# Three products of key halves, a partly on-chip tail and a reordered transition in a cross-attention and stream-mixing kernel

## Chip, cores and metric

The kernel runs on one core of a Trainium2 chip. The metric is the device time of one execution in microseconds (us). Its engines are PE (TensorE, matrix products, with its weight loads listed apart as PEld), DVE (VectorE), ACT (ScalarE), POOL (GpSimd) and SP (SyncE, which here issues every DMA).

## What is computed

For 16 batches of x and ctx, each 256 rows (channels) by 2048 columns, all in float32:

```
x = x + xattn(layernorm(x), ctx)      # layernorm over the 2048 columns
  qh = Wq x ; kh = Wk ctx ; vh = Wv ctx            # 512 = 8 heads of 64
  qh = softmax over the 64 of a head ; kh = softmax over the 2048 columns
  out = Wo (heads' context^T qh) + bo ; x += out / norm(out) * g * 16
x = x + ffn(layernorm(x))             # every row is 4 streams of 512
  24 logits a row (W_res, W_pre, W_post), 50 Sinkhorn rounds on the 4x4 part
  y = (sum of streams * pre) @ W_branch
  out = H_res mixed streams + post * y
```

## The kernel before

The batches are done one behind the other (`for b in range(NB)`), and each batch has a written-out order of **places** that all five engine programs walk through. A batch has 32 key places, `("A", b, r, i)` and `("B", b, r, i)` for r = 0..3 (a block of 128 of the 512 key channels) and i = 0..3 (a quarter of 512 columns), and then 27 query places `("Q", b, i)`.

In the A places `key_logits` (line 546) makes the logits of one quarter, two float32 matmuls of 128x128 by 128x512 into the bank `big[i]`. DVE takes the maxima (`key_max`, line 773, and `key_max_all`, line 780), ACT exponentiates in the B places (`key_exp`, line 1129). PE turns the exponentials round (`key_transpose`, line 557), ACT copies them out (`turn`, line 1138), PE multiplies them by the transposed context (`key_context`, line 571). In the query places follow query logits (line 603), their softmax on DVE, ACT and POOL (lines 857 to 879, 1143, 1346, 1354), transposes (613), the attention product (628), the norm (1154, 887, 1364, 897), the sum with x on POOL (1371) and its return to rows (647, 650, 1161). The key logits of the first block (r = 0) of the next batch are made already in query places 16, 17, 21 and 23; their common maximum is taken behind the last query place and their exponentials in the next batch's B places.

Other work is hung on places by the table `tasks` (`put(place, ...)`): statistics of x (`stat`, line 800; `mean`), the centring of x by ACT (`center`, line 1167) with the scaled weights `wqs` by POOL (line 1330), the small `norm`, `logits` and `pre` steps of the batch before, its branch product y (`y`, lines 1174, 1049, 662, 670), the Sinkhorn steps (`sink`, five groups of 4, 4, 4, 2 and 2 batches), and the `mix`: 24 rows of four streams and y are loaded from DRAM with their coefficients, multiplied by a 121x96 matrix on PE (line 681), copied by ACT (line 1195) and stored. Behind the last batch (place TAIL) come its norm, logits, pre and y, then the Sinkhorn steps of the last group (2 batches, 512 rows) with the mixes still open between them, and then the 22 mixes of this group. Every engine works its program in order, so a wait holds back all that stands behind it on that engine.

## Time and profile before

| | |
|---|---|
| median of 3 runs | 2906.38 us (2905.24 to 2907.76) |
| the profiled execution's own time | 2906.39 us |
| its span, first to last instruction | 2904.7 us |
| mean granted TensorE clock | 0.967 |
| busy: PE / PEld / DVE / ACT / POOL | 2626.9 / 1735.8 / 1663.3 / 1033.0 / 804.3 us |

"L546" is line 546 of the kernel. A row of a group of instructions gives the engine, the operation, the tiles it writes and reads with their shapes, the count, the busy time in us and the mean length of one in ns, and the idle time of the engine ahead of them with what ended it. A row of the timeline gives start and length in us. The names `big`, `tb`, `kc_bank` and `misc` are PSUM banks.

### The profile page before, as it was taken

The numbers are of one execution on the slowest core, as the hardware profiler recorded it, in microseconds if no ns is written. First come the engines' busy times: TensorE is split into PE (matmuls) and PEld (weight loads), VectorE is DVE, ScalarE is ACT, GpSimd is POOL, SyncE is SP. The second block draws the span as 40 slices with busy tenths as digits, with TensorE's granted clock in tenths as the row PEclk, the third lists the DMA queues.
The fourth block names the chain that finished last, engine by engine and source line by source line (L and its number), as shares of the span: only waits on it lengthen the run. The fifth ranks groups of instructions, "written<-read, shape, count | busy, mean of one in ns | idle before, by whom it ended". The sixth has DMA issues, their size and how long they took to land.

```text
span 2904.7 us, 32933 instructions
## 1 busy us (share of the span) xinstructions
PE 2626.9 (90%) x11002; PEld 1735.8 (60%) x11002; DVE 1663.3 (57%) x4194; ACT 1033.0 (36%) x2312; POOL 804.3 (28%) x785
## 2 busy tenths in 40 slices
PE   7989898999989898999989999898998999999765
PEld 4766666666656566565666656566665566656411
DVE  2444434345766757355664766534587685867482
ACT  2333333334332333434333343333434333343222
POOL 1322314050422304142231513214051141512311
PEclk9999999999999999999999999999999999999878
DMA  6112121203112120413324221232413324231166
GB/s 223 37 55 91 58 95 54 92 22 107 39 55 91 59 95 29 140 61 105 120 76 128 70 89 64 82 121 67 137 61 104 122 71 133 69 100 32 52 180 169
DMA packets 203082, 258.22 MB, mean 89 GB/s; under 512 B 45218, under 2 KB 111522, under 8 KB 202914
## 3 DMA queue, kind: packets, MB, share of 16 engines
q1 hardware_dynamic: 202914, 256.12, 28.0%
q8 instruction: 88, 1.44, 0.2%
q14 instruction: 80, 0.66, 0.1%
HBM read 180.17 MB, written 75.89 MB: 88 GB/s over the span
## 4 chain that ended last, share of the span: by engine, by line
PE 77%; DVE 14%; ACT 3%; issue 2%; DMA 1%; POOL 1%; SPq 1%; DVEq 0%; ACTq 0%; POOLq 0%
PE big L628 16%; PE kc_bank L571 15%; PE big L546 13%; PE big L603 13%; PE tb L670 4%; PE tb L613 4%; PE tb L557 4%; PE misc L650 3%; PE tb L681 3%; DVE stats L800 2%; ACT turned L1138 2%; PE kc_bank L647 2%; DVE ska L974 1%; DVE skr L977 1%; DMA out<-mix_out 1%
## 5 line engine op out<-in xcount | busy, mean ns | idle before, releaser
L1138 ACT COPY turned<-tb 128x512 f32<-128x512 f32 x512 | 297.8, 585 | 1021.1 <-PE tb L613 692.7
L546 PE MATMUL big<-ctx_sb,wk 128*128 128x512 f32 x1024 | 515.2, 632 | 50.3 <-ACT k_exp L1129 50.1
L628 PE MATMUL big<-merged,turned 128*128 128x256 f32 x2048 | 492.9, 383 | 61.7 <-ACT turned L1138 61.1
L628 PEld LDWEIGHTS big<-merged,turned 128*128 128x128 f32 x2048 | 380.5, 190 | 206.5 <-issue 123.6
L571 PE MATMUL kc_bank<-ctxt,turned 128*128 128x256 f32 x2048 | 481.8, 379 | 6.8 <-ACT turned L1138 6.8
L603 PE MATMUL big<-wqs,x_sb 128*128 128x512 f32 x1024 | 482.0, 596 | 5.5 <-DVE q_sb L867 4.7
L1346 POOL TENSOR_TENSOR qhalf<-q_sb 128x512 f32<-128x512 f32 x128 | 162.2, 1267 | 922.4 <-ACT q_sb L1143 922.4
L571 PEld LDWEIGHTS kc_bank<-ctxt,turned 128*128 128x128 f32 x2048 | 372.3, 190 | 60.7 <-issue 20.1
L546 PEld LDWEIGHTS big<-ctx_sb,wk 128*128 128x128 f32 x1024 | 195.0, 202 | 246.2 <-issue 173.0
L773 DVE TENSOR_REDUCE kmax<-big 128x1 f32<-128x512 f32 x256 | 173.8, 686 | 286.3 <-PE big L546 285.6
L1354 POOL TENSOR_TENSOR q_sb<-q_sb,qsum 128x1024 f32<-128x1024 f32 x128 | 243.3, 1901 | 332.1 <-DVE qsum L879 332.1
L681 PE MATMUL tb<-mix_ld,mix_w 121*96 121x512 f32 (+2 forms) x346 | 205.7, 690 | 95.9 <-POOL mix_w L1336 66.0
L603 PEld LDWEIGHTS big<-wqs,x_sb 128*128 128x128 f32 x1024 | 180.7, 191 | 155.4 <-issue 145.8
L887 DVE TENSOR_SCALAR nrm<-nrm 128x2 f32<-128x2 f32 x128 | 72.1, 563 | 250.3 <-ACT squares L1154 250.2
L795 DVE TENSOR_SCALAR chain_raw<-kc_bank,ksum 128x256 f32<-128x256 f32 x64 | 31.0, 484 | 314.3 <-PE kc_bank L571 314.0
L857 DVE TENSOR_REDUCE qmax<-big 128x8 f32<-128x512 f32 x256 | 176.3, 689 | 49.1 <-PE big L603 43.4
L867 DVE TENSOR_TENSOR q_sb<-big,qmax 128x512 f32<-128x512 f32 x256 | 169.4, 662 | 52.2 <-PE tb L613 49.7
L1129 ACT ACTIVATE k_exp<-big,kmax 128x512 f32<-128x512 f32 x256 | 175.7, 688 | 53.1 <-DVE kmax L780 53.1
L1371 POOL TENSOR_TENSOR x_tr<-x_tr,on 128x512 f32<-128x512 f32 x128 | 164.7, 1287 | 55.2 <-DVE on L897 55.2
L800 DVE BATCH_NORM_STATS2 stats<-x_sb 128x6 f32<-128x512 f32 x256 | 163.9, 683 | 23.6 <-ACT x_sb L1161 17.0
L1143 ACT ACTIVATE q_sb<-q_sb 128x1024 f32<-128x1024 f32 x128 | 135.4, 1058 | 101.6 <-DVE q_sb L867 101.6
L1195 ACT COPY mix_out<-tb 96x512 f32<-96x512 f32 (+2 forms) x173 | 100.0, 578 | 190.7 <-PE tb L681 140.8
(124 smaller groups left out, 3090.7 us busy)
## 6 DMA issues: line engine op xcount, KB each, us to landing
mix_ld<-streams SPq DMA_DIRECT2D x168, 240.0 KB
ctx_sb<-in_ctx SPq DMA_DIRECT2D x64, 512.0 KB, 9.2
ctxt<-in_ctx_t SPq DMA_DIRECT2D x64, 512.0 KB, 4.6
x_sb<-in_x SPq DMA_DIRECT2D x64, 512.0 KB, 9.0
x_tr<-in_x_t SPq DMA_DIRECT2D x64, 512.0 KB, 6.4
streams<-x_sb SPq DMA_DIRECT2D x64, 512.0 KB, 2.9
out<-mix_out SPq DMA_DIRECT2D x168, 192.0 KB, 2.2
streams<-y_sb SPq DMA_DIRECT2D x32, 256.0 KB, 2.0
```

The lines of the kernel that those rows point to most:

```text
L546: t = nc.tensor.matmul(big[i], wk[:, ct, dt * P:(dt + 1) * P], ctx_sb[b % 2][:, ct, quarter(i)], start=ct == 0, stop=ct == CT - 1)
L571: t = nc.tensor.matmul(kc_bank[:, 0:C], turned[n % 3][:, j * P:(j + 1) * P], ctxt[:, nt, :], start=nt == 0, stop=nt == NT - 1)
L603: t = nc.tensor.matmul(big[i % 2], x_sb[b % 2][:, ct, i * P:(i + 1) * P], wqs[:, ct, :], start=ct == 0, stop=ct == CT - 1)
L628: t = nc.tensor.matmul(big[2 + p % 2][:, half], turned[n % 3][:, dt * P:(dt + 1) * P], merged[:, dt, :], start=dt == 0, stop=dt == DT - 1)
L681: t = nc.tensor.matmul(bank[0:count * STREAMS, :], weights, mix_ld[k][0:ONES + 1, :], start=True, stop=True)
L773: nc.vector.tensor_reduce(kmax[:, 1 + i:2 + i], big[i], AX_X, ALU.max).then_inc(s_kmax, 1)
L800: t = nc.vector.bn_stats(target[:, ct, i, :], x_sb[b % 2][:, ct, quarter(i)])
L857: nc.vector.tensor_reduce(qmax[:, i % 2, :], big[i % 2].rearrange(heads, d=DIM_HEAD), AX_X, ALU.max).then_inc(s_qmax, 1)
L867: nc.vector.tensor_tensor(q_sb[p % QB][:, i % 2, :].rearrange(heads, d=DIM_HEAD), big[i % 2].rearrange(heads, d=DIM_HEAD), qmax[:, i % 2, ...
L1129: nc.scalar.activation(k_exp[:, i * BANK:(i + 1) * BANK], big[i], ACT.Exp, bias=kmax[:, 0:1], accum_out=ksum[:, i:i + 1]).then_inc(s_kexp, 1)
L1138: nc.scalar.copy(turned[k % 3][:], tb[n % 2][:]).then_inc(s_tba, 1)
L1354: nc.gpsimd.tensor_tensor(exps, exps, qsum[:, p % 2, 1, :].unsqueeze(2).broadcast_to([P, 2 * HEADS, DIM_HEAD]), ALU.mult).then_inc(s_qn, 1)
```

## The change

**Key logits.** The weights of the keys and the context are no longer kept in float32: ACT rounds each to a tile of type float32r (`wk_h`, `ctx_h`), POOL subtracts it from the original and keeps the rest, again as float32r (`wk_l`, `ctx_l`). `key_logits` becomes six matmuls: h·h, h·l and l·h for each half of the 256 channels; l·l is left out. The context comes by quarters into two `stage` tiles; loading, rounding and subtracting are tasks of the last key places and of query places 0 to 11.

**Transition.** `key_max_all` of the next batch's first block stands behind its last maximum (query place 24), its first exponential on ACT behind query place 25. The statistics of x move from key places 4 to 7 to 9, 11, 14 and 15, `mean` to 16, `center` to 18 to 27, and `pre` of the batch before to 7, 8 and 9.

**x normalised.** ACT's centring now also multiplies by 1/sigma (`scale=r1`, with `shift1` = -mean/sigma from DVE); POOL's scaling of the query weights (`wqs`) is gone.

**Tail.** The last batch's `pre` and `y` tasks stand between the Sinkhorn steps, one behind every fourth. Of the last group only its first batch goes through the mixes (11 tiles for 22). The last batch is mixed from what is on the chip: ACT makes 8 tiles of 128x512 (`own_first`), DVE adds four terms to each (`own_pair`), SP stores them. `LOADS` goes from 6 to 5.

```diff
-                 for n, size in enumerate(GROUPS)]
-    LOADS, AHEAD = 6, 4
+                 for n, size in enumerate((*GROUPS[:-1], GROUPS[-1] - 1))]
+    LOADS, AHEAD = 5, 4
...
-            put(keys[4 + i], "stat", b, i)
-        put(keys[9], "mean", b)
+            put(keys[(9, 11, 14, 15)[i]], "stat", b, i)
+        put(keys[16], "mean", b)
         for ct in range(CT):
             for i in range(NQ):
-                put(keys[11 + 8 * ct + 2 * i], "center", b, ct, i)
-        put(keys[12], "wq", b)
+                put(keys[(18, 19, 21, 23, 24, 25, 26, 27)[ct * NQ + i]], "center", b, ct, i)
+        put(keys[17], "shift", b)
         if b:
             put(keys[13], "load x_t", b)
         if b + 1 < NB:
             put(keys[25], "load", b + 1)
+
+            for i in range(NQ):
+                put(keys[28 + i] if i < 2 else ("Q", b, 3 * i - 3), "ctx", b + 1, i, -1)
+                for ph in range(1 + CT):
+                    put(("Q", b, 3 * i + ph), "ctx", b + 1, i, ph)
         if b:
-            put(keys[4], "pre", b - 1, 0)
-            put(keys[5], "pre", b - 1, 1)
-            put(keys[6], "pre", b - 1, 2)
+            put(keys[7], "pre", b - 1, 0)
+            put(keys[8], "pre", b - 1, 1)
+            put(keys[9], "pre", b - 1, 2)
             for ct in range(CT):
                 for ph in range(6):
...
+        if n % 4 == 3 and behind_tail:
+            put(TAIL, *behind_tail.pop(0))
...
+                n = b * NQ + i
+                if n >= 2:
+                    w.wait_ge(s_cl, (n - 1) * CT)
+                elif n:
+                    w.wait_ge(s_wkl, 1)
+                nc.sync.dma_start(stage[i % 2][:],
                                   ctx[b].rearrange("(t p) n -> p t n", p=P)[:, :, quarter(i)]).then_inc(s_ctx[i], 16)
 
...
-                    w.wait_ge(s_small[7], 16)
-                    w.wait_ge(s_ctx[i], (b + 1) * 16)
+                    w.wait_ge(s_wkl, 1)
+                    w.wait_ge(s_cl, (b * NQ + i + 1) * CT)
                     if b and i < 2:
                         w.wait_ge(s_qsub, (b - 1) * NT + NT - 1 + i)
                     elif b:
                         w.wait_ge(s_scl, ((b - 1) * PAIRS + PAIRS - 3 + i) * 2)
+                cols = slice(dt * P, (dt + 1) * P)
                 for ct in range(CT):
-                    t = nc.tensor.matmul(big[i], wk[:, ct, dt * P:(dt + 1) * P], ctx_sb[b % 2][:, ct, quarter(i)],
-                                         start=ct == 0, stop=ct == CT - 1)
+                    nc.tensor.matmul(big[i], wk_h[:, ct, cols], ctx_h[:, ct, quarter(i)], start=ct == 0, stop=False)
+                    nc.tensor.matmul(big[i], wk_h[:, ct, cols], ctx_l[:, ct, quarter(i)], start=False, stop=False)
+                    t = nc.tensor.matmul(big[i], wk_l[:, ct, cols], ctx_h[:, ct, quarter(i)], start=False, stop=ct == CT - 1)
                 t.then_inc(s_kl, 1)
 
             def key_transpose(b, dt, i):
@@ -598,9 +636,9 @@
                 else:
...
+                w.wait_ge(s_small[8], 16)
                 for ct in range(CT):
-                    t = nc.tensor.matmul(big[i % 2], x_sb[b % 2][:, ct, i * P:(i + 1) * P], wqs[:, ct, :], start=ct == 0,
+                    t = nc.tensor.matmul(big[i % 2], x_sb[b % 2][:, ct, i * P:(i + 1) * P], wq[:, ct, :], start=ct == 0,
                                          stop=ct == CT - 1)
                 t.then_inc(s_ql, 1)
...
+            def own_pair(n):
+
+                for j in range(1, PARTS):
+                    for k in range(2 * n, 2 * n + 2):
+                        ct, i = k // STREAMS, k % STREAMS
+                        source = x_sb[(NB - 1) % 2][:, ct, quarter(j)] if j < STREAMS else y_sb[ct][:]
+                        if j == 1:
+                            w.wait_ge(s_first, k + 1)
+                        else:
+                            w.wait_ge(s_added, 8 * n + 2 * (j - 2) + k % 2 + 1)
+                        if j == STREAMS:
+                            w.wait_ge(s_tba, SCALAR_READS["y", NB - 1, ct])
+                        nc.vector.scalar_tensor_tensor(
+                            out=own[k], in0=source, scalar=coef_all[:, own_tile + ct, j, i:i + 1], in1=own[k],
+                            op0=ALU.mult, op1=ALU.add).then_inc(s_added, 1)
+
...
+                    if b + 1 < NB and i == 24:
+                        key_max_all(b + 1, 0)
                     behind(place)
-                if b + 1 < NB:
-                    key_max_all(b + 1, 0)
             read_banks(order_of_places[-1])
             behind(TAIL)
...
-                nc.scalar.activation(rows, rows, ACT.Identity, bias=neg_m1[:, ct:ct + 1]).then_inc(s_cent, 1)
+                nc.scalar.activation(rows, rows, ACT.Identity, bias=shift1[:, ct:ct + 1], scale=r1[:, ct:ct + 1]).then_inc(s_cent, 1)
+
+            def context_high(b, i):
+                w.wait_ge(s_ctx[i], (b + 1) * 16)
+                if b:
+                    w.wait_ge(s_kl, kl_count(b - 1, DT - 1, i))
+                nc.scalar.copy(ctx_h[:, :, quarter(i)], stage[i % 2][:]).then_inc(s_ch, 1)
...
+            def own_first(k):
+                ct, i = k // STREAMS, k % STREAMS
+                w.wait_ge(s_skd, len(GROUPS) * SK_STEPS)
+                nc.scalar.activation(own[k], x_sb[(NB - 1) % 2][:, ct, quarter(0)], ACT.Identity,
+                                     bias=bias_all[:, own_tile + ct, i:i + 1],
+                                     scale=coef_all[:, own_tile + ct, 0, i:i + 1]).then_inc(s_first, 1)
...
+                        if r or i or not b:
+                            key_exp(b, r, i)
...
+                    if b + 1 < NB and i == STEPS - 2:
+                        key_exp(b + 1, 0, 0)
...
-            def scale_wq(b):
-                w.wait_ge(s_r1, b + 1)
-                w.wait_ge(s_small[8], 16)
+            def context_low(b, i, ct):
+                w.wait_ge(s_ch, b * NQ + i + 1)
                 if b:
-                    w.wait_ge(s_ql, b * NT)
+                    w.wait_ge(s_kl, kl_count(b - 1, DT - 1, i))
+                nc.gpsimd.tensor_tensor(ctx_l[:, ct, quarter(i)], stage[i % 2][:, ct, :], f32(ctx_h[:, ct, quarter(i)]), ALU.subtract).then_inc(s_cl, 1)
+
+            w.wait_ge(s_wkh, 1)
+            nc.gpsimd.tensor_tensor(wk_l[:], stage[1][:], f32(wk_h[:]), ALU.subtract).then_inc(s_wkl, 1)
+            for i in range(NQ):
                 for ct in range(CT):
-                    nc.gpsimd.tensor_scalar(wqs[:, ct, :], wq[:, ct, :], r1[:, ct:ct + 1], None, ALU.mult).then_inc(s_wq, 1)
+                    context_low(0, i, ct)
```

The first place is ACT's program where batch 1 ends and batch 2 begins, with no Sinkhorn or mix tasks yet: L1138 (now L1199) is `turn`, L1154 (L1215) the squares, L1161 (L1222) the return of rows, L1129 (L1190) the key exponential, L1254 (L1328) the `pre` exponential. Before:

```order
L1138 COPY turned<-tb 128x512
L1154 ACTIVATE squares,nrm<-big 128x256 x2
L1161 COPY x_sb<-kc_bank 128x2x256 x3
L1129 ACTIVATE k_exp,ksum<-big,kmax 128x512
L1254 ACTIVATE pre<-pre 128x8
L1129 ACTIVATE k_exp,ksum<-big,kmax 128x512 x3
```

and now:

```order
L1199 COPY turned<-tb 128x512
L1215 ACTIVATE squares,nrm<-big 128x256 x2
L1222 COPY x_sb<-kc_bank 128x2x256 x2
L1190 ACTIVATE k_exp,ksum<-big,kmax 128x512
L1222 COPY x_sb<-kc_bank 128x2x256
L1190 ACTIVATE k_exp,ksum<-big,kmax 128x512 x3
L1328 ACTIVATE pre<-pre 128x8
L1241 ACTIVATE x_pre<-x_sb,nmur_all,pre 128x512
```

One key exponential of block 0 now stands ahead of the last return of rows, and the other three ahead of the `pre` exponential.

The second place is DVE's program at the same transition: L773 (L811) is the maximum of a quarter of the key logits, L780 (L818) their common maximum, L800 (L838) the statistics of x (those ahead of L805, now L843, are of the batch that ends), L849 (L890) the last row of `logits`. Before:

```order
L800 BN_STATS stats<-x_sb 128x6 x2
L780 TENSOR_REDUCE kmax<-kmax 128x1
L805 BN_AGGR mv<-stats 128x2 x2
...
L849 SCALAR_TENSOR_TENSOR lg<-raw,rr,base_rows 128x24 x2
L800 BN_STATS stats<-x_sb 128x6 x2
L1029 TENSOR_REDUCE pre_s<-lg 128x2
L1031 TENSOR_TENSOR pre<-lg,pre_s 128x8
...
L800 BN_STATS stats<-x_sb 128x6 x2
L785 TENSOR_REDUCE ksum<-ksum 128x1
L787 RECIPROCAL ksum<-ksum 128x1
L773 TENSOR_REDUCE kmax<-big 128x1
```

and now:

```order
L811 TENSOR_REDUCE kmax<-big 128x1 x2
L818 TENSOR_REDUCE kmax<-kmax 128x1
L838 BN_STATS stats<-x_sb 128x6 x2
L843 BN_AGGR mv<-stats 128x2 x2
...
L890 SCALAR_TENSOR_TENSOR lg<-raw,rr,base_rows 128x24 x2
L1070 TENSOR_REDUCE pre_s<-lg 128x2
L1072 TENSOR_TENSOR pre<-lg,pre_s 128x8
...
L811 TENSOR_REDUCE kmax<-big 128x1
L838 BN_STATS stats<-x_sb 128x6 x2
```

The common maximum now stands ahead of the last statistics of the old batch, and no statistics of the new x stand between `logits` and the next key maximum.

The third place is ACT's program over the first query places of a batch (L1204 is the query exponential), as it is now; before, the rows of L1234 were not there:

```order
L1199 COPY turned<-tb 128x512 x2
L1234 CAST ctx_h<-stage 128x2x512
L1204 ACTIVATE q_sb<-q_sb 128x1024
L1234 CAST ctx_h<-stage 128x2x512
L1204 ACTIVATE q_sb<-q_sb 128x1024
L1199 COPY turned<-tb 128x512 x2
L1204 ACTIVATE q_sb<-q_sb 128x1024
L1199 COPY turned<-tb 128x512
L1234 CAST ctx_h<-stage 128x2x512
L1215 ACTIVATE squares,nrm<-big 128x256 x2
```

Four casts of 128x1024 stand between the turns and the exponentials of the query softmax, each behind its DMA.

The last place is the head of SP's program as it is now (before, `stage` read `ctx_sb` and `wk`, and none of these DMAs waited):

```order
L430 DMA stage<-in_ctx 128x2x512
L537 DMA stage<-in_wk_t 128x2x512
L430 DMA stage<-in_ctx 128x2x512 x3
L537 DMA bo_heads<-in_bo 128x256
L537 DMA base_rows<-in_base 128x24
L537 DMA g_rows<-in_g 128x256
```

The order of the DMAs is unchanged, but the second context quarter now waits for POOL's subtraction of the weights and the third and fourth for those of the first and second quarter, with all others queued behind them.

## Rows read from the trace of the kernel before

**Rows 1.** The page: busy time of PE, and its granted clock in 40 slices.

```profile
PE 2626.9 (90%) x11002; PEld 1735.8 (60%) x11002; DVE 1663.3 (57%) x4194; ACT 1033.0 (36%) x2312; POOL 804.3 (28%) x785
...
PEclk9999999999999999999999999999999999999878
```

**Rows 2.** Windows, batch 2 (keys, queries), 8 (keys): busy PE, PEld, DVE, ACT, POOL.

```profile
350.20:415.50 65.30, 65.30 (x281) 44.91 (x281) 20.12 (x45) 26.34 (x54) 5.05 (x4) 1.00 0.26 88
415.50:510.70 95.20, 86.28 (x386) 59.69 (x385) 51.16 (x114) 31.00 (x73) 40.88 (x33) 0.96 0.17 57
1343.20:1416.10 72.90, 72.66 (x298) 47.94 (x297) 34.38 (x90) 31.45 (x68) 6.94 (x10) 1.00 0.43 137
```

**Rows 3.** Timeline, PEld: weight loads of the key logits, one a record.

```profile
34.92 0.19 PEld L546 LDWEIGHTS big<-ctx_sb,wk 128*128 128x128 f32 x1 [0.24 <-issue]
35.35 0.19 PEld L546 LDWEIGHTS big<-ctx_sb,wk 128*128 128x128 f32 x1 [0.24 <-issue]
```

**Rows 4.** Groups by line, PE: the records of the key logits.

```profile
L546 PE MATMUL big<-ctx_sb,wk 128*128 128x512 f32 x1024 | 515.2, 632 | 50.3 <-ACT k_exp L1129 50.1
```

**Rows 5.** Timeline, PE: bursts of transposes, context products and the maps.

```profile
338.20 0.97 PE L650 MATMUL misc<-wmap,x_tr 128*128 128x24 f32 x8
...
356.05 0.60 PE L557 MATMUL tb<-ident,k_exp 128*128 128x128 f32 x4
356.49 1.89 PE L571 MATMUL kc_bank<-ctxt,turned 128*128 128x256 f32 x8
358.22 0.60 PE L557 MATMUL tb<-ident,k_exp 128*128 128x128 f32 x4
```

**Rows 6.** Timeline, PE and ACT: batch 1 has ended, batch 2 begins.

```profile
341.20 0.69 ACT L1129 ACTIVATE k_exp<-big,kmax 128x512 f32<-128x512 f32 x1 [1.41 <-DVE kmax L780]
...
342.03 2.86 PE L546 MATMUL big<-ctx_sb,wk 128*128 128x512 f32 x4 [2.86 <-ACT k_exp L1129]
...
345.69 0.21 ACT L1254 ACTIVATE pre<-pre 128x8 f32<-128x8 f32 x1 [3.72 <-DVE pre L1031]
...
362.55 1.88 PE L546 MATMUL big<-ctx_sb,wk 128*128 128x512 f32 x4
```

**Rows 7.** Timeline, PE: the same transition into batch 8, with mixes.

```profile
1338.15 1.99 PE L681 MATMUL tb<-mix_ld,mix_w 121*96 121x512 f32 x2 [4.15 <-POOL mix_w L1336]
```

**Rows 8.** Groups by line, POOL, ACT and DVE.

```profile
L1371 POOL TENSOR_TENSOR x_tr<-x_tr,on 128x512 f32<-128x512 f32 x128 | 164.7, 1287 | 55.2 <-DVE on L897 55.2
...
L1143 ACT ACTIVATE q_sb<-q_sb 128x1024 f32<-128x1024 f32 x128 | 135.4, 1058 | 101.6 <-DVE q_sb L867 101.6
...
L1049 DVE SCALAR_TENSOR_TENSOR x_pre<-x_sb,pre,x_pre 128x512 f32<-128x512 f32 x96 | 73.3, 764 | 11.9 <-ACT x_pre L1174 9.7
```

**Rows 9.** Source lines 887 and 972: length in ns, shortest, median, longest.

```profile
L887 DVE TENSOR_SCALAR nrm<-nrm x128: 104/456/1546, 115.0 to 2722.3; 128x2 f32<-128x2 f32 x128
...
L972 DVE TENSOR_TENSOR skw<-skp,skb x220: 210/281/1668, 682.9 to 2849.5; 128x128 f32<-128x128 f32 x66, 128x64 f32<-128x64 f32 x44
```

**Rows 10.** Timeline, DVE, PE, SP and ACT: the tail.

```profile
2735.21 0.54 DVE L849 SCALAR_TENSOR_TENSOR lg<-raw,rr,base_rows 128x24 f32<-128x24 f32 x2
...
2759.14 0.22 DVE L947 TENSOR_REDUCE ska<-skp 128x16 f32<-128x64 f32 x1 [7.02 <-ACT skp L1204]
...
2856.10 0.43 SPq L463 DMA_DIRECT2D coef_rows<-coef  x1
...
2863.17 6.47 PE L681 MATMUL tb<-mix_ld,mix_w 121*96 121x512 f32 x8 [15.81 <-POOL mix_w L1336]
...
2902.03 0.57 ACT L1195 COPY mix_out<-tb 32x512 f32<-32x512 f32 x1 [0.94 <-DMA out<-mix_out]
```

**Rows 11.** DMA issues and timeline: landing of the key weights, PE's first work.

```profile
wk<-in_wk_t SPq DMA_DIRECT2D x1, 512.0 KB, 5.4
...
15.19 7.00 PE L688 MATMUL misc<-wmap,chain_t 128*128 128x24 f32 x32 [15.19 <-DMA wmap<-in_w_maps_t]
22.01 8.87 PE L546 MATMUL big<-ctx_sb,wk 128*128 128x512 f32 x16
```

85 lines of the change are left out of this document (59 added, 26 removed).

## Prediction

> **What bounds the kernel now.** The page comes first. PE is busy for 2626.9 us of 2904.7, and its clock reads 9 tenths or more until the last slices [rows 1]; the next engine, DVE, stands at 57%. The windows say in which stage this holds. In the key places of batch 2 PE is busy for all of 65.3 us and DVE for 20.1; in the query places it is 86.3 of 95.2 us; in a batch that carries Sinkhorn steps and mixes (batch 8) the key places have PE at 72.7 of 72.9 us with DVE at 34.4 [rows 2]. So a PE instruction saved in a key place is time saved. The windows of batch 2 make 160.5 us; the tail behind the last batch's `logits` takes 169.5 us [rows 10], and there PE is not the bound.
>
> The sum is made against the profiled execution (2906.39 us, span 2904.7); it stands within 0.01 us of the median, 2906.38. A difference of 0.2%, 5.8 us, is about what a measurement of this kernel can tell from none.
>
> **Key logits.** A float32 matmul shows as two records, and 1024 records stand for 512 matmuls [rows 4]. The weight loads of successive records follow each other by 35.35 - 34.92 = 0.43 us [rows 3]: 512 columns at 2.4 GHz are 0.213 us, so a record streams every column twice. One call of `key_logits` has four records, 1.72 us. It gets six products of float32r, of which this trace shows none. From below: if one product streams its columns once, it takes as long as a record of 256 columns streamed twice, and those follow each other by (358.22 - 356.49) / 8 = 0.216 us, each with a weight load of its own hidden behind it [rows 5]. That gives 6 x 0.216 = 1.30 us a call. From above: two streams, as a float32 record, 6 x 0.43 = 2.58 us. I take the lower value, because two records of two streams make four partial products, and the change asks for three of four. The one row against it is the transpose, a single record of 128 columns at (356.49 - 356.05) / 4 = 0.11 us, twice its 0.053 us of columns; but eight records of only 24 columns take 0.97 us, 0.12 each [rows 5], so that price is one of loading weights and not of columns.
>
> The Trainium skill (FP8 and Floating Point Precision, TensorE Precision Notes) says that true float32 is four passes, H·H, H·L, L·H and L·L, and reduced float32 a single one at some 22 bits. By it the call would be 1.30 us, as taken. The two records of 0.43 us agree with the four passes; no row here shows the single one.
>
> The saving is 0.42 us x 256 calls = 107 us. Three calls in four stand in key places, where PE has no gap, and count in full (80 us); the fourth stands in query places 16 to 23, where PE idles about a tenth, and I count half (14 us). **-94 us**; bounds -107 and, if DVE's and ACT's chain sets part of the pace of the shorter key places, -60.
>
> **Transition.** When batch 1 ends PE stops at 338.20 + 0.97 = 339.17 us [rows 5]. The first exponential comes at 341.20, behind the common maximum that waited for the last statistics; the others come behind `pre`, for which ACT idles 3.72 us [rows 6]. PE reaches the logits of block 2 at 362.55 us, 23.4 us later, with 16.0 us of work in between (four calls at 1.72, twenty transposes at 0.11, four groups of eight context records at 1.73). So 7.4 us are lost, part of it as half clock. In the new order the first exponential stands ahead of the last return, and the other three need nothing from DVE; I expect 6 of the 7.4 us back. In batches with mixes PE is held 4.15 us by `mix_w` instead, which waits behind POOL's `norm` and so behind DVE's statistics [rows 7]; this stays, and there I take 3 us. With seven transitions of the first kind and eight of the second: **-66 us**, bounds -30 (1 to 3 us each) and -105 (7 each).
>
> **Query places.** ACT gets four casts of 128x1024 a batch, 1.06 us each by the query exponential of that size; POOL gets eight subtractions of 128x512 at 1.29 us, 10.3 us a batch, and loses the two of `wqs` [rows 8]. In the query places POOL works 40.9 of 95.2 us and ACT 31.0 [rows 2], so both have room, but these copies stand between turns and exponentials for which PE waits. I charge half a us a batch, **+8 us**; bounds 0 and +32 (2 us a batch, some half of the casts uncovered). Centring keeps its one ACT instruction and nothing is charged; `mix_w` no longer stands behind `wqs` on POOL in the key places, **-2 us**. The fifth load buffer gone costs nothing, as only four loads run ahead. `shift` holds DVE until POOL's power is done, with key maxima behind it, which is covered by a context group of 1.73 us.
>
> DVE's small instruction on `nrm` takes 104 ns at its shortest and 456 in the median, one Sinkhorn product 210 and up to 1668 [rows 9]: DVE is held at times in this stage. The Trainium skill (SBUF — State Buffer, Who interferes with whom) says that DVE and GpSimd share a read interface, and that a DVE instruction with two SBUF inputs blocks against a GpSimd one that reads SBUF. If all of the subtractions' 10.3 us a batch were lost by it, the sum would stand 147 us higher, at 2877.
>
> **Tail.** `logits` are ready at 2735.21, but Sinkhorn's first sum on DVE waits 7.02 us, until 2759.14, for an exponential, since ACT stands at y; the coefficients are stored at 2856.10 [rows 10], so 97 us of Sinkhorn follow. Now they begin at 2736 and take with them six DVE additions of 0.76 us [rows 8] and some waits, about 8 us: 2841, **-15 us**. Behind them 22 mixes end at 2904.7, 48.6 us. Of these 7 us pass before the first (2863.17), and from there 22 copies take 39 us to 2902.03, 1.77 us each. Eleven take 19.5, so this path ends 7 + 19.5 + 2.5 = 29 us behind the coefficients. The own tiles: one ACT instruction, then 32 DVE additions of 0.764 us = 24.4, plus 1 and a store of 3: 28.5 us. They share the DMA engines, so I say 31 instead of 48.6: **-17 us**. Bounds of the tail as a whole -22 and -38.
>
> **Head.** PE makes its first key logits at 22.01 us [rows 11]. Now the chain is: the weights land about 7 us in (5.4 us from issue [rows 11]), a cast of 1.06, a subtraction of twice 1.29, so quarter 1 is issued near 11 us; its landing, taken as 5.4 us too, its cast and its two subtractions take 9 us, and only then, near 20 us, is quarter 3 issued, with all small loads behind it. The map weights among them are what PE waits for first, until 15.19 us now; they would land near 26 us. So PE starts some 11 us later, of which a little comes back where x or the transposed context was late anyway. **+10 us**, bounds +5 and +16.
>
> Sum: -94 - 66 + 8 - 2 - 32 + 10 = -176 us, so **2730 us**. All bounds on the good side give -107 - 105 + 0 - 2 - 38 + 5 = -247 (2659), all on the bad side -60 - 30 + 32 - 22 + 16 = -64 (2842); both at once are unlikely.
>
> **Rivals.**
> 1. *The key places become bound by the exponential chain* (maximum, common maximum, exponentials, turns). For it: after a block's last logits come two maxima on DVE and four exponentials of 0.69 us [rows 6] on ACT, with turns between. Against it: 6.9 us of context products cover them, and DVE is busy 34 of 73 us [rows 2]. Then the logits give 40 us and transitions 50: 2906 - 40 - 50 + 8 - 2 - 32 + 10 = 2800. Chance 0.12.
> 2. *A float32r product streams twice.* It would be slower than before: 2.58 instead of 1.72 us, +0.86 x 256 = +220 us; with the rest unchanged 2906 + 220 - 66 + 8 - 2 - 32 + 10 = 3044. It decides from 0.34 us a product on, (1.72 + 82 / 256) / 6, as the other terms give 82 us. For it stands only the transpose's 0.11 us; against it the count of records. If a product were even run as a full float32 matmul, so that the change doesn't do what it says, it would be +878 us. Chance of both 0.08.
> 3. *The query places stall*: casts, subtractions and held DVE instructions cost 3 us a batch, +45 instead of +8: 2767. For it the held instructions [rows 9], against it POOL's idle half [rows 2]. Chance 0.14.
>
> The forecast keeps 0.66. The range, 2665 to 2820, takes in the forecast's bounds short of their joint ends and rivals 1 and 3, and leaves out rival 2 and some of the edges. Faster: 0.66 + 0.12 + 0.14, less 0.01 for no change: 0.91. Same 0.01, slower 0.08.
>
> **What would show it.** Right: 1536 records of key products about 0.22 us apart; PE resuming within 1 us of the last return in batch 2; Sinkhorn beginning within 2 us of `logits`; some 31 us behind the last coefficients; PE's first key logits near 33 us. Wrong: products 0.43 us apart, PE waiting in the key places for `k_exp`, or in query places 0 to 11 for `turned`.

## The result and the profile after the change

The changed kernel takes **2837.84 us** (median of 4 runs, 2834.25 to 2839.26), the kernel before 2906.39 us beside it: ratio 0.9761, 95% interval 0.9747 to 0.9776. It is faster by 68.5 us, not by the 176 us forecast, and the time lies above the range (2665 to 2820). The profiled execution has a span of 2836.7 us against 2904.7 us.

The lines of the page and of its groups that answer to [rows 1, 4]; the first has busy us, share and instructions, a group has count, busy us, mean ns, idle time before it and what ended most of it:

```profile
PE 2528.3 (89%) x11492; PEld 1838.4 (65%) x11492; DVE 1715.8 (60%) x4226; ACT 1103.8 (39%) x2374; POOL 921.2 (32%) x870
...
PEclk9999999999999999999999999999999999999976
...
L609 PE MATMUL kc_bank<-ctxt,turned 128*128 128x256 f32 x2048 | 492.2, 385 | 32.5 <-ACT turned L1199 32.5
...
L583 PE MATMUL big<-ctx_h,wk_h 128*128 128x512 f32 x512 | 250.6, 489 | 28.5 <-ACT k_exp L1190 28.4
...
L584 PE MATMUL big<-ctx_l,wk_h 128*128 128x512 f32 x512 | 208.4, 407 | 0.0
L585 PE MATMUL big<-ctx_h,wk_l 128*128 128x512 f32 x512 | 208.0, 406 | 0.0
```

TensorE's idle time for exponentials fell (50.3 us ahead of `L546` before [rows 4], 28.5 ahead of `L583` now), but its idle time for the copies `turned`, ahead of the context products, rose from 6.8 to 32.5 us. Most of those waits are new.

**Where the time went, by stage.** A batch is measured from TensorE's last `maps` record of one batch to that of the next; the tail runs from there. All in us:

| stretch | before | after | saved |
|---|---|---|---|
| batch 0 (with the head) | 180.1 | 184.6 | -4.5 |
| batches 1 to 3 (no Sinkhorn, no mixes) | 480.0 | 459.4 | 20.6 |
| batches 4 to 7 | 672.0 | 657.2 | 14.8 |
| batches 8 to 11 | 689.1 | 672.9 | 16.2 |
| batches 12 to 15 (densest in both) | 706.9 | 702.0 | 4.9 |
| from the last `maps` to the end | 176.6 | 160.6 | 16.0 |

The light batches save 6.9 us each, batches 4 to 11 3.9 each, the last four 1.2. The forecast had products and transitions win 160 us (94 + 66), some 10 a batch.

**The products.** Timeline of TensorE in batch 2, start and length of one record each:

```profile
339.94 0.40 PE L584 MATMUL big<-ctx_l,wk_h 128*128 128x512 f32 x1
...
340.17 0.40 PE L585 MATMUL big<-ctx_h,wk_l 128*128 128x512 f32 x1
...
340.40 0.40 PE L583 MATMUL big<-ctx_h,wk_h 128*128 128x512 f32 x1
```

At the full clock a product follows the one before by 0.23 us, not 0.216; over the 16 steps from 338.54 to 342.27 us it is 0.233. A call takes 1.40 us instead of 1.72, which is 0.32 us won and not 0.42. So at most 82 us stood to be won (256 calls at 0.322; the expectations below, with 1.395 us a call, say 83), not 107. The single stream itself was right, against a float32 record's 0.43 us [rows 3]. The Trainium skill (FP8 and Floating Point Precision, TensorE Precision Notes) has four passes for true float32 and lets reduced float32 be cut to the width that TensorE multiplies at; a single stream agrees with that, and for its interval the page has no figure. What takes the 0.017 us more than a float32 stream of as many columns is not shown.

**The transition.** Start of batch 2, which answers to [rows 6]:

```profile
337.37 0.69 ACT L1190 ACTIVATE k_exp<-big,kmax 128x512 f32<-128x512 f32 x1 [1.82 <-DVE kmax L818]
...
338.20 0.50 PE L583 MATMUL big<-ctx_h,wk_h 128*128 128x512 f32 x1 [0.54 <-ACT k_exp L1190]
...
344.57 1.28 DVE L838 BATCH_NORM_STATS2 stats<-x_sb 128x6 f32<-128x512 f32 x2
345.76 0.15 DVE L1080 TENSOR_TENSOR pre<-pre,pre_s 128x8 f32<-128x8 f32 x1
...
346.15 0.81 ACT L1241 ACTIVATE x_pre<-x_sb,nmur_all,pre 128x512 f32<-128x512 f32 x1 [2.48 <-DVE pre L1082]
346.87 1.05 ACT L1199 COPY turned<-tb 128x512 f32<-128x512 f32 x2
...
347.58 3.48 PE L609 MATMUL kc_bank<-ctxt,turned 128*128 128x256 f32 x8 [2.65 <-ACT turned L1199]
```

The early exponential works: TensorE waits 0.54 us where it waited 2.86 [rows 6]. But the block ends sooner than ScalarE is ready. ScalarE stands at the start of `x_pre`, for which it needs `pre`; VectorE's last step on `pre` shares place 9 with the first statistics, which are put ahead of it (1.28 us, behind a key maximum of 0.67). Behind `x_pre` stand the copies, and for them TensorE now idles 2.65 us. The eight context records behind take 3.48 us instead of 1.89 [rows 5]: the window of that group (columns below) has a granted clock of 0.56, near the lower of the two levels, 1.2 GHz, after an idle stretch at whose end the clock still read 1.00:

```profile
345.00:347.50 2.50, 0.00 (x0) 0.00 (x0) 2.46 (x7) 1.35 (x3) 0.00 (x0) 1.00 1.05 351
347.60:350.00 2.40, 2.40 (x7) 1.93 (x8) 2.33 (x6) 1.00 (x3) 0.00 (x0) 0.56 0.07 22
```

(length, then busy us of PE, PEld, DVE, ACT, POOL, granted clock, DMA share, GB/s.) From the last `maps` (337.66) to the logits of block 2 (357.37) pass 19.7 us. Work in it is 14.7 (16.0 less four calls at 0.32), so 5.0 us are still lost, where the forecast left 1.4.

With Sinkhorn steps the same place is worse. Start of batch 5:

```profile
811.92 0.29 DVE L1017 TENSOR_TENSOR skw<-skp,ska 128x128 f32<-128x128 f32 x1
...
815.39 0.17 DVE L1072 TENSOR_TENSOR pre<-lg,pre_s 128x8 f32<-128x8 f32 x1
...
816.12 0.35 DVE L1015 RECIPROCAL ska<-skr 128x32 f32<-128x32 f32 x1
...
819.20 0.81 ACT L1241 ACTIVATE x_pre<-x_sb,nmur_all,pre 128x512 f32<-128x512 f32 x1 [3.40 <-DVE pre L1082]
...
820.63 0.77 PE L609 MATMUL kc_bank<-ctxt,turned 128*128 128x256 f32 x1 [7.69 <-ACT turned L1199]
```

From 811.92 to 816.47 us VectorE does Sinkhorn steps, with the pre weights between them; then follow a key maximum and the statistics, and TensorE has waited 7.69 us. The transitions into batches 6 and 10 have such a wait too, of 8.37 and 7.13 us.

Into batches 4, 7 and 11 TensorE waits for an exponential instead, 5.13, 6.18 and 5.96 us. Start of batch 4:

```profile
650.30 0.31 ACT L1278 ACTIVATE skp<-skp 128x128 f32<-128x128 f32 x1 [5.34 <-DVE skp L985]
...
651.34 0.79 PE L583 MATMUL big<-ctx_h,wk_h 128*128 128x512 f32 x1 [5.13 <-ACT k_exp L1190]
```

A group's first Sinkhorn step has an exponential on ScalarE (`skp`), its coefficients another (`coef`, into batches 7 and 11). Each needs `logits` from VectorE and stands ahead of the key exponentials, so these wait for VectorE after all.

**Windows, and a reading of mine that was off.** The windows of [rows 2] were laid 11 us too late: batch 2 begins at 339.2 us, as [rows 6] show, not at 350.2. So the "key places without a gap" left out the transition, the very place the change is about. Laid rightly, the keys of batch 2 and of batch 5 in the kernel before:

```profile
339.20:404.50 65.30, 60.74 (x245) 39.96 (x246) 25.54 (x67) 28.60 (x62) 5.15 (x5) 0.95 0.34 113
...
826.40:893.90 67.50, 60.31 (x246) 39.59 (x246) 39.41 (x113) 28.79 (x65) 5.37 (x5) 0.97 0.33 109
```

and in the changed kernel the keys of batch 2 and the transition into batch 5 alone:

```profile
337.60:396.90 59.30, 56.11 (x270) 44.85 (x270) 25.50 (x66) 28.94 (x62) 2.04 (x3) 0.97 0.32 107
...
804.20:820.60 16.40, 6.74 (x32) 5.33 (x33) 13.80 (x47) 4.88 (x13) 1.36 (x2) 0.84 0.50 160
```

In the kernel before, TensorE is idle for 4.6 and 7.2 us of these key places, where [rows 2] showed 0.0 (batch 2) and 0.2 (batch 8). Over them VectorE is busy for 39 and 58% of the time (31 and 47% in the windows of [rows 2]); in the 16.4 us of the changed kernel's transition it is busy for 13.8 and TensorE for 6.7.

**The tail**, which answers to [rows 10], timeline of DVE, SP, POOL and PE:

```profile
2683.77 0.20 DVE L982 TENSOR_SCALAR skz<-lg 128x64 f32<-128x64 f32 x1
...
2786.11 0.43 SPq L492 DMA_DIRECT2D coef_rows<-coef  x1
...
2786.91 4.06 DVE L1096 SCALAR_TENSOR_TENSOR k_exp<-x_sb,coef,k_exp 128x512 f32<-128x512 f32 x6 [0.95 <-ACT k_exp L1267]
...
2793.07 16.24 POOL L1426 TENSOR_TENSOR mix_w<-mix_mask,mix_co 120x96 f32<-120x96 f32 x4 [17.24 <-DMA mix_w<-bias_rows]
...
2808.54 3.70 PE L719 MATMUL tb<-mix_ld,mix_w 121*96 121x512 f32 x4 [31.55 <-POOL mix_w L1426]
```

Sinkhorn begins at once, and the coefficients are stored 102.9 us behind `logits` (2683.18) instead of 120.9: 18 us, 15 forecast. Behind them the end comes after 50.6 us, where the forecast had 31 and the kernel before 48.6. VectorE's 32 additions run back to back from 2786.91 to 2808.2 us. GpSimd's first matrix has its loads at 2793.07. The 16.24 us of the row are one instruction of 15.33 us, the longest of its line, and three of 0.34 behind it; the median of all 162 is 0.35. The long one ends at 2808.40, 0.2 us behind the last addition, and TensorE mixes nothing until 2808.54. The Trainium skill (SBUF — State Buffer, Who interferes with whom) has the rule: a VectorE instruction with two SBUF inputs blocks against a GpSimd one that reads SBUF. The trace agrees that the two exclude each other, but the matrix was held through 22 further additions and not through one. The prediction named the rule for the query places and did not ask where else it holds.

**The head**, which answers to [rows 11], timeline of SP and PE:

```profile
9.73 7.78 SPq L430 DMA_DIRECT2D stage<-in_ctx  x3
...
19.48 0.43 SPq L537 DMA_DIRECT2D wmap<-in_w_maps_t  x1
...
26.57 7.00 PE L726 MATMUL misc<-wmap,chain_t 128*128 128x24 f32 x32 [26.57 <-DMA wmap<-in_w_maps_t]
33.39 0.77 PE L583 MATMUL big<-ctx_h,wk_h 128*128 128x512 f32 x1
```

The first key logits come at 33.39 us instead of 22.01, as worked out. By the end of batch 0, which has gains of its own, the changed kernel is 4.5 us late.

### The profile page after: what moved, and what is told of

Its sections match the earlier page's. It is cut to its first block, busy times and chain, and to the rows that moved or that the text cites. A ratio compares the mean times of both kernels' runs of the same rounds, so it can differ in the third digit from the quotient of the medians.

```text
span 2836.7 us, 34124 instructions
## 1 busy us (share of the span) xinstructions
PE 2528.3 (89%) x11492; PEld 1838.4 (65%) x11492; DVE 1715.8 (60%) x4226; ACT 1103.8 (39%) x2374; POOL 921.2 (32%) x870
## 4 chain that ended last, share of the span: by engine, by line
PE 72%; DVE 17%; ACT 3%; issue 3%; POOL 2%; DMA 1%; SPq 0%; DVEq 0%; POOLq 0%; ACTq 0%
PE big L666 15%; PE kc_bank L609 15%; PE big L641 13%; PE tb L651 4%; PE tb L708 4%; PE tb L595 3%; PE big L583 3%; PE big L585 3%; PE big L584 3%; PE tb L719 3%; PE misc L688 3%; DVE stats L838 2%; ACT turned L1199 2%; PE kc_bank L685 1%; DVE ska L1015 1%
## 5 line engine op out<-in xcount | busy, mean ns | idle before, releaser
L1199 ACT COPY turned<-tb 128x512 f32<-128x512 f32 x512 | 297.6, 586 | 937.0 <-PE tb L651 660.0
L609 PE MATMUL kc_bank<-ctxt,turned 128*128 128x256 f32 x2048 | 492.2, 385 | 32.5 <-ACT turned L1199 32.5
L641 PE MATMUL big<-wq,x_sb 128*128 128x512 f32 x1024 | 486.5, 600 | 5.9 <-DVE q_sb L908 5.1
L609 PEld LDWEIGHTS kc_bank<-ctxt,turned 128*128 128x128 f32 x2048 | 379.0, 194 | 89.4 <-issue 46.4
L1414 POOL TENSOR_TENSOR ctx_l<-stage,ctx_h 128x512 fp32r<-128x512 f32 x128 | 164.1, 1283 | 602.5 <-ACT ctx_h L1234 602.5
L811 DVE TENSOR_REDUCE kmax<-big 128x1 f32<-128x512 f32 x256 | 174.6, 686 | 225.9 <-PE big L585 224.9
L719 PE MATMUL tb<-mix_ld,mix_w 121*96 121x512 f32 (+2 forms) x324 | 192.0, 692 | 105.1 <-POOL mix_w L1426 85.6
L641 PEld LDWEIGHTS big<-wq,x_sb 128*128 128x128 f32 x1024 | 181.5, 192 | 157.4 <-issue 146.8
L583 PE MATMUL big<-ctx_h,wk_h 128*128 128x512 f32 x512 | 250.6, 489 | 28.5 <-ACT k_exp L1190 28.4
L928 DVE TENSOR_SCALAR nrm<-nrm 128x2 f32<-128x2 f32 x128 | 90.7, 708 | 219.4 <-ACT squares L1215 219.1
L584 PE MATMUL big<-ctx_l,wk_h 128*128 128x512 f32 x512 | 208.4, 407 | 0.0
L585 PE MATMUL big<-ctx_h,wk_l 128*128 128x512 f32 x512 | 208.0, 406 | 0.0
L1190 ACT ACTIVATE k_exp<-big,kmax 128x512 f32<-128x512 f32 x256 | 176.1, 690 | 54.0 <-DVE kmax L818 54.0
L838 DVE BATCH_NORM_STATS2 stats<-x_sb 128x6 f32<-128x512 f32 x256 | 163.0, 681 | 19.7 <-ACT x_sb L1222 19.0
```

The lines of the kernel that those rows point to most:

```text
L583: nc.tensor.matmul(big[i], wk_h[:, ct, cols], ctx_h[:, ct, quarter(i)], start=ct == 0, stop=False)
L584: nc.tensor.matmul(big[i], wk_h[:, ct, cols], ctx_l[:, ct, quarter(i)], start=False, stop=False)
L585: t = nc.tensor.matmul(big[i], wk_l[:, ct, cols], ctx_h[:, ct, quarter(i)], start=False, stop=ct == CT - 1)
L609: t = nc.tensor.matmul(kc_bank[:, 0:C], turned[n % 3][:, j * P:(j + 1) * P], ctxt[:, nt, :], start=nt == 0, stop=nt == NT - 1)
L641: t = nc.tensor.matmul(big[i % 2], x_sb[b % 2][:, ct, i * P:(i + 1) * P], wq[:, ct, :], start=ct == 0, stop=ct == CT - 1)
L719: t = nc.tensor.matmul(bank[0:count * STREAMS, :], weights, mix_ld[k][0:ONES + 1, :], start=True, stop=True)
```

## The experiments

All are edits of the changed kernel and are compared with the kernel before, run on the same chip. To put them beside one another each ratio is taken times 2906.4 us; the changed kernel stands at 0.9761, 2837 us, in that measure.

| run | ratio [95% interval] | us against the change |
|---|---|---|
| a1_whole | 0.9963 [0.9949, 0.9977] | +58.7 |
| b1_places | 0.9834 [0.9819, 0.9848] | +21.2 |
| c1_tail | 0.9822 [0.9808, 0.9837] | +17.7 |
| d1_nostage | 0.9715 [0.9701, 0.9729] | -13.4 |
| d2_nosub | 0.9726 [0.9713, 0.9738] | -10.2 |
| m1_pre | 0.9766 [0.9749, 0.9784] | +1.5 |
| m1_sink | 0.9731 [0.9716, 0.9746] | -8.7 |
| m2_own | 0.9703 [0.9688, 0.9719] | -16.9 |
| h1_head | 0.9709 [0.9694, 0.9724] | -15.1 |
| m3_all | 0.9617 [0.9604, 0.9630] | -41.9 |
| m3_skip | 0.9709 [0.9695, 0.9722] | -15.1 |
| m4_best | 0.9558 [0.9545, 0.9570] | -59.0 |

An interval is about 4 us to either side, and a difference between two rows is sure to about 6 us. Lengths of stretches from the traces, us:

| kernel | batch 0 | 1-3 | 4-7 | 8-11 | 12-15 |
|---|---|---|---|---|---|
| changed | 184.6 | 459.4 | 657.2 | 672.9 | 702.0 |
| a1_whole | 190.7 | 466.2 | 674.3 | 690.4 | 713.3 |
| b1_places | 190.5 | 466.0 | 660.7 | 680.1 | 702.2 |
| d1_nostage | 183.7 | 456.3 | 655.5 | 669.4 | 695.8 |
| d2_nosub | 184.3 | 459.3 | 656.3 | 669.9 | 695.6 |
| m1_pre | 185.1 | 452.6 | 657.4 | 675.8 | 704.4 |
| m1_sink | 184.4 | 452.7 | 639.3 | 672.6 | 719.6 |
| h1_head | 172.9 | 457.8 | 657.4 | 672.9 | 702.0 |
| m3_all | 172.8 | 452.6 | 638.1 | 680.0 | 707.6 |
| m3_skip | 172.5 | 452.7 | 638.0 | 690.0 | 726.5 |
| m4_best | 169.7 | 452.7 | 638.0 | 667.5 | 700.2 |

### The products undone

```diff
 for ct in range(CT):
-    nc.tensor.matmul(big[i], wk_h[:, ct, cols], ctx_h[:, ct, quarter(i)], start=ct == 0, stop=False)
-    nc.tensor.matmul(big[i], wk_h[:, ct, cols], ctx_l[:, ct, quarter(i)], start=False, stop=False)
-    t = nc.tensor.matmul(big[i], wk_l[:, ct, cols], ctx_h[:, ct, quarter(i)], start=False, stop=ct == CT - 1)
+    t = nc.tensor.matmul(big[i], f32(wk_h[:, ct, cols]), f32(ctx_h[:, ct, quarter(i)]), start=ct == 0, stop=ct == CT - 1)
```

> The changed kernel with one float32 product a half of ctx_h and wk_h in place of the three of halves (what the low halves add is left out). Theory A, TensorE bounds every batch: a call goes back from 1.395 us to 1.72 us, 256 calls are 83 us, so 2837.8 + 83 = 2921 us. Theory B, in the batches with Sinkhorn steps VectorE ends the waits and a faster product only makes TensorE wait longer: the light batches 0 to 3 lose 5.2 us each, the others about half of that, so about 2837.8 + 21 + 31 = 2890 us, and the gaps between the logits of the second place group shrink in the slow kernel.

The products are worth 58.7 us, of 82 that the records offer: between the theories, nearer B. But the place of the loss is not B's. Batches 4 to 15 slow by 45.9 us, 3.8 each; the light ones by 6.8, only 2.3 each, where B had 5.2. The timeline of TensorE in a1_whole, in batch 2's transition, says why:

```profile
356.46 1.97 PE L607 MATMUL kc_bank<-ctxt,turned 128*128 128x256 f32 x8 [1.36 <-ACT turned L1197]
```

With slower logits TensorE comes later to the same copy, waits 1.36 us instead of 2.65, and keeps its clock: the context group takes 1.97 us instead of 3.48. So in a light batch 1.3 us of idle time and 1.5 of half clock, 2.8 of the 5.2 us that the products saved, went into the transition's new wait.

### The places undone

```diff
-put(keys[(9, 11, 14, 15)[i]], "stat", b, i)
+put(keys[4 + i], "stat", b, i)
...
-put(keys[9], "pre", b - 1, 2)
+put(keys[6], "pre", b - 1, 2)
...
-                    if b + 1 < NB and i == 24:
-                        key_max_all(b + 1, 0)
```

(likewise `mean` back at 9, `shift` at 10, centring from 11, `pre` at 4 and 5; the maximum stands behind the last step again, the first exponential in its old place.)

> The changed kernel with the keys' first places as they were: statistics at places 4 to 7, mean at 9, centring from 11, pre weights at 4 to 6, the maximum over quarters behind the last query step and the first exponential in its old place. Theory A (the forecast): the new places are worth 66 us, so 2904 us. Theory B (from the trace after): the exponentials start early but TensorE then waits 2.65 us for the copy of the transposes, so a light batch kept only 2.1 us of the 6 and a Sinkhorn batch nothing: 2837.8 + 4 x 2.1 = 2846 us. Rival C: the old order is faster in the Sinkhorn batches, because the statistics no longer stand with the pre weights: under 2837.

21 us, a third of the forecast's 66. Its timeline, again into batch 2, has the old waits back, 2.86 and 1.65 us, in place of 0.54 and 2.65:

```profile
349.07 0.80 PE L583 MATMUL big<-ctx_h,wk_h 128*128 128x512 f32 x1 [2.86 <-ACT k_exp L1190]
...
353.66 0.50 PE L583 MATMUL big<-ctx_h,wk_h 128*128 128x512 f32 x1 [1.65 <-ACT k_exp L1190]
```

Theory B's 2.1 us a light batch is met (6.6 in three), and 5.9 us more lie in batch 0, which B had left out. Batches 4 to 7 and 8 to 11 give 3.5 and 7.2 us, batches 12 to 15 nothing.

### The tail undone

```diff
-    for n, size in enumerate((*GROUPS[:-1], GROUPS[-1] - 1))]
+    for n, size in enumerate(GROUPS)]
...
-        if n % 4 == 3 and behind_tail:
-            put(TAIL, *behind_tail.pop(0))
```

(`pre` and `y` stand ahead of Sinkhorn again, the own pairs and their stores are gone.)

> The changed kernel with the tail as it was: 22 mixed tiles of the last two batches through DRAM, pre weights and y ahead of Sinkhorn, no additions on chip. Theory A (the forecast): 32 us slower, 2870 us. Theory B (from the trace after: 18 us won ahead of the coefficients, 2 us lost behind them): 16 us slower, 2854 us, with the first Sinkhorn step about 18 us later behind the last logits and 48.6 us from the coefficients' store to the end, against 50.6 us.

Theory B: 17.7 us, little more than half of what was forecast. In its trace the coefficients are stored 122.4 us behind `logits` and the end comes 49.7 us later; in the changed kernel it is 102.9 and 50.6.

### The staging taken out

d1_nostage leaves out loads, casts and subtractions of the context behind batch 0, so every later batch takes batch 0's halves; d2_nosub leaves out the subtractions alone, so every later batch takes its own high halves and batch 0's low ones. The edit of d2_nosub, without the waits that go with it:

```diff
-                for ph in range(1 + CT):
+                for ph in range(1):
                     put(("Q", b, 3 * i + ph), "ctx", b + 1, i, ph)
```

> The changed kernel without loads, casts and subtractions of the context behind batch 0 (every batch takes batch 0's halves; so 15 x 4 loads and casts and 15 x 8 subtractions are left out). Theory A: ScalarE and GpSimd have the room in the query places, nothing or at most 0.5 us a batch comes back: 2830 to 2838 us. Theory B, GpSimd's subtractions are paid in the query places: 1.3 us for each of 4 pairs, about 5 us a batch, 2760 us. The normalisation steps of VectorE that took 786 ns beside GpSimd would be fewer in B.

> The changed kernel without GpSimd's subtractions behind batch 0 (120 of 128 left out; ctx_l stays that of batch 0); loads and casts stay. d1_nostage, which left out all of the staging, was 15 us faster. Theory A, that cost is GpSimd's, whose 1.27 us instructions delay the norm steps between VectorE and GpSimd: nearly all of it comes back, 2823 to 2827 us. Theory B, it is ScalarE's casts of 1.04 us ahead of turns and exponentials: 2835 to 2838 us.

The staging costs 13.4 us, between the theories of d1_nostage and far nearer A, and 10.2 of it come back without the subtractions, as A of d2_nosub has it: most of the cost is GpSimd's part. What loads and casts take beyond that, 3.2 us, is within the intervals. Of the subtractions' cost 9.4 us lie in batches 8 to 15 and hardly any in 1 to 7. VectorE's small instruction on `nrm`, the one of [rows 9] (456 ns in the median there), has in the changed kernel, and then without the subtractions (line 932 there), in ns, shortest, median, longest:

```profile
L928 DVE TENSOR_SCALAR nrm<-nrm x128: 104/716/1547, 121.7 to 2671.3; 128x2 f32<-128x2 f32 x128
```

```profile
L932 DVE TENSOR_SCALAR nrm<-nrm x128: 104/448/1547, 121.7 to 2660.9; 128x2 f32<-128x2 f32 x128
```

This line takes 16.4 us more in the changed kernel, while the total is 10 us longer, not the 147 us that stood in the prediction for all of the subtractions' time. The Trainium skill's rule for two SBUF inputs (SBUF — State Buffer, Who interferes with whom) does not cover this instruction, which has one; the same section lets a `tensor_scalar`, as this is, exclude GpSimd only in its two-port modes, and no run shows in which mode it ran. All other instructions of VectorE together take 5.2 us more beside the subtractions; the lines that grow most, Sinkhorn's on `sku` and `skw` (5.9 us), have two inputs. That so little of the worst case came is put down to VectorE's time to spare in these places; no run isolates it.

### The new wait of the transition

```diff
-put(keys[(9, 11, 14, 15)[i]], "stat", b, i)
+put(keys[(10, 11, 14, 15)[i]], "stat", b, i)
...
-put(keys[((10, 12, 13, 14, 15, 16), (18, 20, 21, 22, 23, 24))[ct][ph]], "y", b - 1, ct, ph)
+put(keys[((12, 13, 14, 15, 16, 17), (18, 20, 21, 22, 23, 24))[ct][ph]], "y", b - 1, ct, ph)
```

> The changed kernel with the second first-statistics pair behind the pre weights (place 10 in place of 9) and the start of x_pre on ScalarE moved from place 10 to 12, behind the first exponential and turn of that group. Theory A, the wait for the copy of the transposes (32.5 us in 8 places, and TensorE at half clock behind each) is the change's new wait and comes from this queue: in the light batches it goes whole, 2.65 us and 1.7 us of half clock, so 3 to 4 us in each of three transitions; in Sinkhorn batches VectorE is 4.5 us late anyway and the wait moves on to the exponentials, 0 to 3 us each. Together 10 to 25 us: 2815 to 2829 us. Rival B, the exponential chain ends the second place group anyway: 2838 us.

No gain in the total: rival B's number, and a miss for A. In the light batches it works, 2.3 us each (459.4 to 452.6), and the wait is a shorter one with another cause; timeline of m1_pre into batch 2:

```profile
347.55 0.69 ACT L1190 ACTIVATE k_exp<-big,kmax 128x512 f32<-128x512 f32 x1 [3.76 <-DVE kmax L818]
...
348.95 3.82 PE L609 MATMUL kc_bank<-ctxt,turned 128*128 128x256 f32 x16 [1.45 <-ACT turned L1199]
```

It is the common maximum now, late on VectorE. Into batches 5, 6 and 10 that wait fell too, from 7.69, 8.37 and 7.13 us to 1.95, 4.15 and 2.92, and these three batches together are no shorter (491.2 us against 491.0): the time went into other waits, for `x_pre` and `chain_raw` among them. Batches 8 to 15 are 5.3 us longer; whether by the later y or by the moved statistics was not tried. The next run takes Sinkhorn steps off the places in question:

```diff
-free = [place for place in order_of_places[starts[gr]:starts[gr + 1] - 8] if place[0] != "A"]
+free = [place for place in order_of_places[starts[gr]:starts[gr + 1] - 8] if place[0] != "A" and place[::2] != ("B", 0)]
```

> m1_pre, and Sinkhorn steps kept off the four places 4 to 7 of a batch, where VectorE does norm rows, logits and pre weights. Theory A, VectorE's queue in the transition ends the waits of the Sinkhorn batches: 4 to 5 us come back in each of 8 to 11 transitions, 20 to 50 us below m1_pre's time of about 2822: 2775 to 2802 us. Rival B, the steps that move crowd VectorE elsewhere as much: the time of m1_pre, within 5 us.

In the total neither: 8.7 us below the change, 10.2 below m1_pre, where A had 20 and more. Batches 4 to 7 win 18.1 us against m1_pre, most of it in batches 4 and 7 (5.2 and 6.4), where in m1_pre the key logits still wait for the exponentials behind Sinkhorn's. Timeline of m1_pre into batch 4, which has no such wait in m1_sink:

```profile
644.96 0.79 PE L583 MATMUL big<-ctx_h,wk_h 128*128 128x512 f32 x1 [5.12 <-ACT k_exp L1190]
```

In batch 5 the wait at the first context group, 7.69 us in the changed kernel and 1.95 in m1_pre, is 1.09 in m1_sink, so most of that gain was m1_pre's:

```profile
803.57 1.97 PE L609 MATMUL kc_bank<-ctxt,turned 128*128 128x256 f32 x8 [1.09 <-ACT turned L1199]
```

In batches 12 to 15, whose groups have half as many places for the same number of steps, it costs 15.2 us. There VectorE has less room anywhere, busy for 502 of 702 us in the changed kernel, where it is 409 of 657 in batches 4 to 7; that this is the reason is likely and not tried.

### Tail and head mended

```diff
+                        if j == 1 and k % 2 == 0 and n:
+                            w.wait_ge(s_blk, len(mix_tiles) - len(MIX_TILES[LAST]) + 1 + 3 * n)
                         if j == 1:
                             w.wait_ge(s_first, k + 1)
```

> The changed kernel; in the tail VectorE's additions of own pair 1, 2 and 3 wait until GpSimd has made 4, 7 and 10 of the 11 mixing matrices. Theory A, VectorE's 32 additions back to back kept GpSimd out (a matrix record of 16 us against 0.3 us each): from the coefficients' store to the end 50.6 us becomes about 36 us, 2824 us. Rival B, the loads of the mixing rows were what GpSimd waited for: no change, 2838 us.

16.9 us for a wait that was added, and theory A is met. The mixes now run beside the additions; from the coefficients' store (2785.45) to the end of the span (2821.7) it is 36.3 us, as expected. GpSimd's first matrix, timeline of m2_own:

```profile
2792.46 0.35 POOL L1428 TENSOR_TENSOR mix_w<-mix_mask,mix_co 120x96 f32<-120x96 f32 x1 [17.13 <-DMA mix_w<-bias_rows]
```

and TensorE's first mixes, 16 us earlier than in the changed kernel:

```profile
2792.95 6.32 PE L719 MATMUL tb<-mix_ld,mix_w 121*96 121x512 f32 x8 [16.46 <-POOL mix_w L1428]
```

Six of the eleven matrices come in VectorE's pauses and take 0.34 or 0.35 us. The other five come beside additions and take 0.51 to 0.86, the first of them in the middle of a burst that runs from 2796.51 to 2801.99:

```profile
2799.29 0.83 POOL L1428 TENSOR_TENSOR mix_w<-mix_mask,mix_co 120x96 f32<-120x96 f32 x1 [2.81 <-DMA mix_w<-bias_rows]
```

So a burst of additions does not always hold GpSimd until its end, as it did for 15.33 us in the changed kernel. What let this one in is not shown.

The head, where the small loads now stand ahead of the context quarters:

```diff
-            first = 7
-            for i in [first, *[k for k in range(len(small)) if k != first]]:
-                if i == first:
-                    load_ctx(0, 0)
+            load_ctx(0, 0)
+            for i in (7, 0, 1, 2, 3, 4, 5, 6, 8, 9):
+                if i in (6, 8, 9):
+                    load_ctx(0, (6, 8, 9).index(i) + 1)
...
-                if i == first:
-                    for p in range(1, NQ):
-                        load_ctx(0, p)
```

(and the gates' exponential stands ahead of the casts on ScalarE.)

> The changed kernel with the small loads (wmap among them) issued before context quarters 1 to 3, and the gates' exponential before the casts. Theory A, the queue stood at the second quarter (7.8 us for three issues) with the small loads behind it: the first key logits come 8 to 12 us earlier, at about 22 us, and the end 5 to 10 us: 2828 to 2833 us. Rival B, the transfers of ctxt, x and x_t are saturated until 50 us and set when batch 0 goes on: 2836 to 2838 us.

15.1 us, more than the 5 to 10 that A expected, 11.7 of them in batch 0: `wmap` is issued at 3.73 us instead of 19.48, and the first key logits stand at 16.68 us, ahead even of the 22.01 of the kernel before. Timeline of PE:

```profile
9.87 6.99 PE L723 MATMUL misc<-wmap,chain_t 128*128 128x24 f32 x32 [9.87 <-DMA wmap<-in_w_maps_t]
...
16.68 0.77 PE L580 MATMUL big<-ctx_h,wk_h 128*128 128x512 f32 x1
```

### Together

m3_all has h1, m2, m1_pre and the Sinkhorn rule for the first group alone; m3_skip adds `place[::2] != ("A", 0)` to the condition on which a mix is put; m4_best is m3_all with m1_pre's places in batches 0 to 7 alone and the Sinkhorn rule in the first two groups.

> The changed kernel with the edits of m1_pre, m2_own and h1_head, and Sinkhorn steps kept off places 4 to 7 in the first group alone (batches 4 to 6, where m1_sink gained 16 us by the end of batch 7; in batches 12 and 13 it lost 15). Theory A, head, transition and tail are separate stretches and their gains add: 2837.8 - 16 (head) - 16.5 (tail) - 16 (batches 4 to 7) - 7 (batches 1 to 3) + 7 (what batches 8 to 15 gave back in m1_pre) = 2789 us. Rival B, the gains meet the same wait at the end (spills and y of the last batch): above 2800 us.

> m3_all, and no mixing tile is put on places 0 to 3 of a batch, where GpSimd stands at the norm rows of the batch before with the mixing matrices behind it and TensorE waited 4.5 to 7.6 us in six batches. Theory A, that wait is on the path: 20 to 30 us less than m3_all in batches 8 to 15, partly given back since more tiles are left for the tail: 2765 to 2780 us. Rival B, in those batches VectorE is the bound, TensorE waits next for the exponentials or the copies instead: within 5 us of m3_all, the gap before the mixing matmul gone and another in its place.

> m3_all with the key places of m1_pre in batches 0 to 7 alone (the changed kernel's own behind them) and Sinkhorn steps kept off places 4 to 7 in the first two groups. Theory A, from the lengths of batches: batches 8 to 11 took 679.9 us in m3_all and 672.6 in m1_sink, and batches 12 to 15 took 707.6 us against 702.0 in the changed kernel: 2797.5 - 7 - 5 = 2785 us. Rival B, the lengths of neighbouring batches depend on one another and the gain is under 4 us: 2794 to 2798 us.

m3_all was to win 48.5 us by its sum and wins 41.9; its batches 8 to 15 took 1387.6 us, 7.4 more than in m1_pre, from which they were taken, so the miss lies there. That the moved Sinkhorn steps of the first group end later and push what follows is likely, but no run isolates it. m3_skip is a clear miss of both its theories, 27 us slower than m3_all: with the mixes gone from places 0 to 3 the key places of batches 8 to 15 became only 2.7 us shorter in all, so the wait [rows 7] seems to have stood mostly where TensorE would have waited anyway; the query places became 31.7 us longer. Why a mix costs more there was not tried further and stays open. m4_best is the fastest here: **2779.8 us, ratio 0.9558** [0.9545, 0.9570], 59 us below the change by the ratios. Theory A had 2785; of the gain on m3_all 12.5 us lie in batches 8 to 11 and 7.4 in batches 12 to 15.

## Why the prediction was wrong

The direction was right, and the signs of all terms that were tried; the size was not, mostly by two terms and less by the tail.

- **Key logits, -94: measured -58.7.** The step that failed first is the duration of one product, taken as 0.216 us from the context records; it is 0.233, which takes 25 of the 107 us and, counted as the prediction counts, leaves 72. The second is that key places let a saved TensorE instruction count in full: 58.7 came out, and in a light batch 2.8 of 5.2 us went into the wait for `turned` and the half clock behind it. The low bound of -60, named for just this chain of VectorE and ScalarE, is what came.
- **Transition, -66: measured -21.2.** "the other three need nothing from DVE; I expect 6 of the 7.4 us back" is the step that failed. In the light batches the exponentials need nothing, but ScalarE's next instruction, `x_pre`, does, and the copies that TensorE needs stand behind it. The order of the places was there to be read: statistics ahead of `pre` on VectorE at place 9, y at place 10 on ScalarE ahead of the copy. For batches with Sinkhorn steps nothing was subtracted, though VectorE does twelve such instructions in that very stretch, and into batches 4, 7 and 11 an exponential of Sinkhorn's stands ahead of the key exponentials on ScalarE. The windows that lay 11 us late helped to hide it. The value lies outside the bound of -30 too.
- **Tail, -32: measured -17.7.** Sinkhorn ahead was right (18 for 15). "31 instead of 48.6 us" failed: it added up each engine's own work and let additions and matrices run side by side. Run m2_own shows that, with an order that lets them, 36.3 us are reached.
- **Query places, +8: measured +13.4** for all the staging, inside the bounds; 2 us of `wqs` were not tried alone.
- **Head, +10:** the first logits came 11.4 us later, as worked out; h1_head gives 15.1 back.

The measured parts add up, -58.7 - 21.2 - 17.7 + 13.4 + 15.1 = -69.1 us, beside 68.5 to 69.5 measured. They were each taken with the others present, and h1_head gives back more than the change took (its first logits are 5.3 us ahead of the kernel before), so that fit is partly luck. Rival 1, the key places bound by the chain of maxima, exponentials and turns (2800 us), was nearest in kind: it gave products and transitions 90 us together, and they measured 79.9; it still took the tail at its full 32 and the head at 10. Rival 2 is refuted by the records, rival 3 (45 us in the query places) by d1_nostage.

## What to carry to other kernels

Where an instruction is taken off the critical engine, follow each other engine's queue for the next few instructions and ask which one it meets next: here one pair of statistics held a tiny product, that held `x_pre`, that held a copy, and the copy held TensorE, which then ran at half clock. Read windows at the borders that the timeline shows, and the transition by itself: a mean over a stage hides the 16.4 us in which VectorE is busy for 13.8. Two engines' work next to each other is no plan until their orders say how they interleave; an added wait between VectorE and GpSimd won as much in this tail (17 us) as the whole new tail had.

## What the runs showed of the hardware

- A reduced-float32 product of 128x128 by 512 columns follows the next by 0.233 us, a float32 record of the same columns by 0.43 us, a record of 256 columns with float32 operands by 0.216 us. Three products for one float32 matmul of two records are 0.70 us against 0.86. Where the granted clock is 0.50 (b1_places, 349.07 to 351.6 us) the products stand 0.425 us apart, which is 512 columns at 1.2 GHz (0.427).
- Additions of VectorE with two SBUF inputs, back to back for 21 us, kept one GpSimd instruction of usually 0.35 us from completing for 15.33 us, until the last of them. In a pause of VectorE it takes 0.35 us (m2_own). Beside shorter bursts five took 0.51 to 0.86 us; what decides between the two is open.
- TensorE's granted clock fell behind waits of 2.65 us in the transition: the same eight context records take 3.48 us there, 1.97 us behind a wait of 1.36 us in a1_whole, 1.89 us in the steady stretch. So removing such a wait, or shortening it as far as in a1_whole, is worth up to 1.6 us beyond its own length.
